# Graph network kernel, second aggregation pass: counts on four column groups, fourteen block buffers, two blocks kept in place

## The reference, cut to what matters

```python
def hyp_agg(x, src, dst, w, c, n_nodes):          # once in each of the two layers
    xt = logmap0(x, c)
    msg = xt[src] * w[:, None]
    agg = jax.ops.segment_sum(msg, dst, num_segments=n_nodes)
    return proj(expmap0(agg, c), c)
...
edge_features = jnp.concatenate([x[src], x[dst]], axis=-1)
h = jax.nn.relu(edge_features @ W1 + b1)
edge_out = h @ W2 + b2
agg = jax.ops.segment_sum(edge_out, dst, num_segments=n)
counts = jax.ops.segment_sum(jnp.ones_like(dst, dtype=edge_out.dtype), dst, num_segments=n)
return agg / jnp.clip(counts, 1.0)[:, None]
```

## Time and the profile before

| | |
|---|---|
| median of three runs | 1223.57 us (1220.88 to 1223.95) |
| the profiled execution | 1225.43 us |
| its span, first to last instruction | 1223.6 us |
| TensorE busy | 1063.2 us, 87% of the span |
| VectorE busy | 1001.1 us, 82% |
| ScalarE busy | 669.2 us, 55% |
| DMA traffic | 171.75 MB, 140 GB/s over the span |

### The profile page before, as it was taken

One profiled execution on the slowest core, in us unless ns is written; L12 is line 12 of the kernel. 1 busy time (PEld: TensorE's weight loads), 2 busy tenths in 40 slices (PEclk: granted clock), 3 DMA queues, 4 the chain that ended last, 5 costly groups with the idle time before them and its releaser, 6 DMA issues.

```text
span 1223.6 us, 53479 instructions
## 1 busy us (share of the span) xinstructions
PE 1063.2 (87%) x21956; PEld 984.6 (80%) x21956; DVE 1001.1 (82%) x1477; ACT 669.2 (55%) x1837; POOL 27.5 (2%) x28
## 2 busy tenths in 40 slices
PE   2079989898898988559999579999999999999997
PEld 2057877777777777358999559999999999999997
DVE  8789999999999997465554868888888888888884
ACT  5348888888888887300001475555555555555552
POOL 7000000000000000100000000000000000000000
PEclk9579999999999999769999679999999999999999
DMA  2003232222323223439991244444444445444440
GB/s 79 0 32 124 92 122 99 115 118 96 122 92 122 108 106 123 183 140 372 354 371 35 86 149 159 157 156 156 156 156 156 156 157 158 157 158 155 159 149 29
DMA packets 45160, 171.75 MB, mean 140 GB/s; under 512 B 19472, under 2 KB 19798, under 8 KB 45115
## 3 DMA queue, kind: packets, MB, share of 16 engines
q1 hardware_dynamic: 45115, 171.12, 39.2%
HBM read 122.95 MB, written 48.14 MB: 140 GB/s over the span
## 4 chain that ended last, share of the span: by engine, by line
PE 53%; DVE 32%; issue 8%; DVEq 4%; ACT 3%; DMA 0%; POOL 0%; POOLq 0%; ACTq 0%
PE PS L1475 17%; PE PS L1477 11%; DVE arena L985 8%; PE PS L1495 7%; PE PS L1354 7%; DVE arena L962 5%; PE PS L1490 5%; DVE arena L970 4%; DVE arena L948 3%; PE PS L1382 3%; DVE arena L957 2%; DVEq L344 2%; PE PS L1430 1%; DVE Cw L777 1%; DVE rows L777 1%
## 5 line engine op out<-in xcount | busy, mean ns | idle before, releaser
L1475 PE MATMUL PS<-arena 125*128 125x128 bf16 x3600 | 344.9, 219 | 6.3 <-ACT RT L714 6.2
L1475 PEld LDWEIGHTS PS<-arena 125*128 125x128 bf16 x3600 | 250.6, 97 | 11.2 <-issue 7.3
L1354 PE MATMUL PS<-arena,A 125*64 125x72 f32 x4800 | 178.1, 229 | 69.1 <-DVE aggTw L996 40.2
L1354 PEld LDWEIGHTS PS<-arena,A 125*64 125x64 f32 x4800 | 164.4, 138 | 78.7 <-DVE A L866 27.0
L609 ACT ACTIVATE arena<-arena 128x72 bf16<-128x72 bf16 x864 | 216.9, 343 | 2.1 <-DVE arena L970 2.1
L728 ACT ACTIVATE arena<-PS 128x512 bf16<-128x512 f32 (+2 forms) x336 | 172.2, 543 | 82.6 <-PE PS L1477 82.5
L721 ACT ACTIVATE arena<-arena 128x512 bf16<-128x512 f32 x144 | 90.9, 631 | 153.8 <-DVE arena L1198 153.7
L1477 PE MATMUL PS<-arena 108*128 108x128 bf16 x1200 | 167.6, 221 | 0.0
L1477 PE MATMUL PS<-arena,HTw 108*128 108x128 bf16 x1200 | 165.8, 219 | 0.0
L1339 PE MATMUL PS<-arena 128*128 128x72 bf16 x3600 | 126.9, 199 | 0.0
L1339 PEld LDWEIGHTS PS<-arena 128*128 128x128 bf16 x3600 | 120.8, 101 | 4.9
(11 more groups left out here) (188 smaller groups left out, 1458.3 us busy)
## 6 DMA issues: line engine op xcount, KB each, us to landing
adjacency<-arena SPq DMA_DIRECT2D x48, 900.0 KB, 3.6
arena<-adjacency SPq DMA_DIRECT2D x48, 900.0 KB, 4.8
Bw<-slot_rows SPq DMA_DIRECT2D x48, 800.0 KB, 4.1
Cw<-slot_rows SPq DMA_DIRECT2D x48, 700.0 KB, 4.4
arena<-q_table SPq DMA_DIRECT2D x144, 18.0 KB
q_table<-arena SPq DMA_DIRECT2D x6, 336.0 KB
slot_rows<-slot_row SPq DMA_DIRECT2D x49, 13.0 KB
x_sb<-in_x SPq DMA_DIRECT2D x1, 700.0 KB
```

The source lines that it names most:

```text
L1354: last = mm(sums[half, :], A[:, b, :], adjacency[0:PN, b, :], start=(b < 2), stop=(b >= NB - 2))
L1475: mm(ps, OTs[k][:, b, :], P3[:, b, part, :], start=(part == 0), stop=False)
```

## The change

The counts of tile t go to partitions 32 (t mod 4) to 32 (t mod 4) + 31, with 32 columns of ones as the stationary operand, so that four partial counts stand on four quarters of the partitions. `degree` is then all of `RT`, and the product at the end (line 1437) adds the four with the vector `first_of` (ones on partitions 0, 32, 64 and 96), in two halves of the nodes. The counts have two PSUM buffers, and wait for the additions of the group two before. VectorE makes the one-hots of group g + 1 in step g. `OC` and `offb` move from the arena into `Cw`. The arena gives 14 block buffers in place of six. SyncE issues the loads of groups 0 to 5 and then 38 to 45 without waiting, and then those of 6 to 37 through six buffers. Groups 46 and 47 are read from `AB[0]` and `AB[1]`, and not loaded. The order is 6 groups written out, a loop of five iterations over six groups, and 12 groups written out.

```diff
+EARLY = 8
+LOOPED = NG - EARLY - 2
...
-        degree = RT[0:1, :]
+        degree = RT[:, :]
...
+        starts = list(range(0, kept - NB * W + 1, NB * W)) + list(range(at[0], ARENA - NB * W + 1, NB * W))
...
-        cnt_ps = bank(3)[0:1, 0:W]
+        cnt_ps = [bank(2 + k)[:, 0:W] for k in range(2)]
...
-            whole = (NG - SECOND) // SECOND - 1
-            first = NG - whole * SECOND
-            for g in range(first):
+            for g in range(SECOND):
+                body(g, g, 0, g % 2)
+            rounds = LOOPED // SECOND
+            with eng.Fori(1, rounds) as j:
+                for r in range(SECOND):
+                    body(SECOND * j + r, r, j, r % 2)
+            for g in range(rounds * SECOND, LOOPED):
                 body(g, g % SECOND, g // SECOND, g % 2)
-            with eng.Fori(0, whole) as j:
-                for i in range(SECOND):
-                    g = first + i
-                    body(SECOND * j + g, g % SECOND, j + g // SECOND, g % 2)
+            for g in range(LOOPED, NG - 2):
+                body(g, SECOND + g - LOOPED, 0, g % 2)
+            for g in range(NG - 2, NG):
+                body(g, None, 0, g % 2)
...
+            def load_second():
+                for g in range(SECOND):
+                    load_blocks(g, g)
+                for g in range(LOOPED, NG - 2):
+                    load_blocks(g, SECOND + g - LOOPED)
+                rounds = LOOPED // SECOND
+                with sp.Fori(1, rounds) as j:
+                    for r in range(SECOND):
+                        sp.wait_ge(applied2, nth(SECOND * (j - 1) + r))
+                        load_blocks(SECOND * j + r, r)
+                for g in range(rounds * SECOND, LOOPED):
+                    sp.wait_ge(applied2, nth(g - SECOND))
+                    load_blocks(g, g % SECOND)
...
+            ve.tensor_reduce(first_of[:, :], ident[:, 0:128:32], X, ALU.add)
...
-                def body(g, _, n, k):
-                    ve.wait_ge(cone_set, nth(g - 2))
+                def count_onehots(g, k):
+                    ve.wait_ge(counted, nth(g - 2))
                     nc.vector.tensor_copy(offb[k], offT[:, bass.ds(g * GT, GT)].unsqueeze(2)
...
                     ve.wait_ge(cdloc_set, nth(g))
-                    ve.wait_ge(counted, nth(g - 2))
...
+                def body(g, at_k, n, k):
+                    if not is_last(g):
+                        count_onehots(g + 1, 1 - k)
                     base = window(ve, g)
...
-                    nc.vector.tensor_tensor(win, win, cnt_ps, ALU.add).then_inc(added2, 1)
+                    nc.vector.tensor_tensor(win, win, cnt_ps[k], ALU.add).then_inc(added2, 1)
...
-                apply(applied2, agg2_ps[k], ABS[blocks_at])
+                apply(applied2, agg2_ps[k], AB[k] if at_k is None else ABS[at_k])
                 pe.wait_ge(cone_set, nth(g))
-                pe.wait_ge(added2, 2 * g + PRIMED)
+                if from_third(g):
+                    pe.wait_ge(added2, 2 * g - 2 + PRIMED)
                 for t in range(GT):
-                    last = mm(cnt_ps, onesb[:, 0:1], OC[k][:, t, :], start=(t == 0), stop=(t == GT - 1))
+                    quarter = slice(32 * (t % 4), 32 * (t % 4) + 32)
+                    last = mm(cnt_ps[k][quarter, :], onesb[:, 0:32], OC[k][:, t, :], start=(t < 4), stop=(t >= GT - 4))
...
-                last = mm(PS[0:PN, 3584 + b:3585 + b], degree[:, 0:N].rearrange("f (p b) -> f b p", b=NB)[:, b, :],
-                          ones[0:1, 0:1], start=True, stop=True)
+                for ps in node_halves:
+                    last = mm(PS[ps, 3584 + b:3585 + b], degree[:, 0:N].rearrange("f (p b) -> f b p", b=NB)[:, b, ps],
+                              first_of[:, :], start=True, stop=True)
```

More of the change, by code:

```diff
@@ L121, in gnn_kernel @@
         y2s = sb("y2s", [128, 2])
+        first_of = sb("first_of", [128, 1])
         oki = sb("oki", [1, 2], i32)
@@ L150, in gnn_kernel @@
         AB = [carve(NB * W).rearrange("p (b w) -> p b w", w=W) for _ in range(2)]
[L152 to L155, removed]
+        kept = at[0] - 2 * NB * W
+        starts = list(range(0, kept - NB * W + 1, NB * W)) + list(range(at[0], ARENA - NB * W + 1, NB * W))
+        assert len(starts) >= SECOND + EARLY
+        ABS = [arena[:, i:i + NB * W].rearrange("p (b w) -> p b w", w=W) for i in starts[0:SECOND + EARLY]]
+        OC = [Cw[:, i * GT * HW:(i + 1) * GT * HW].bitcast(bf16).rearrange("p (t w) -> p t w", w=W) for i in range(2)]
+        offb = [Cw[:, 2 * GT * HW + i * GT:2 * GT * HW + (i + 1) * GT].bitcast(bf16).rearrange("p (t d) -> p t d", d=2)
+                for i in range(2)]
         fieldT = carve(TILES * FIELDS, bf16).rearrange("p (t f d) -> p t f d", f=FIELDS, d=2)
@@ L272, in gnn_kernel @@
         a_stored = sem("a_stored")
-        a_in = [sem(f"a_in{k}") for k in range(SECOND)]
+        a_in = [sem(f"a_in{k}") for k in range(SECOND + EARLY)]
         applied2, added2, counted, cdloc_set, cone_set = (counts(n) for n in (
@@ L387, in store_rows, with load_blocks @@
                     .then_inc(row_stored, 16)
-            def load_blocks(g, k, n, c):
-                if not (isinstance(g, int) and g < SECOND):
-                    sp.wait_ge(applied2, nth(g - SECOND))
+            def load_blocks(g, k):
                 sp.dma_start(ABS[k].rearrange("p b w -> p (b w)"),
                              a_d[bass.ds(g, 1), :, :].rearrange("g p w -> (g p) w")).then_inc(a_in[k], 16)
+            def load_second():
[11 more added lines that the diff above has]
+                    load_blocks(g, g % SECOND)
             def any_indices(i):
@@ L416, in _ @@
                     with sp.If(fast == 1):
-                        second_groups(sp, load_blocks)
+                        load_second()
             def load_sources(g):
@@ L1058, in body @@
                     win = degree[:, bass.ds(base, W)]
-                    nc.vector.tensor_tensor(win, win, cnt_ps, ALU.add).then_inc(added2, 1)
+                    nc.vector.tensor_tensor(win, win, cnt_ps[k], ALU.add).then_inc(added2, 1)
+                count_onehots(0, 0)
                 second_groups(ve, body)
@@ L1105, in any_order @@
                         if i < 2:
-                            win = degree[:, bass.ds(v * W, W)]
+                            win = degree[0:1, bass.ds(v * W, W)]
                             nc.vector.tensor_tensor(win, win, any_ps[F:F + 1, :], ALU.add)
@@ L1372, in first_body, with second_body @@
                 blocks(g, k)
-            def second_body(g, blocks_at, n, k):
-                pe.wait_ge(a_in[blocks_at], 16 * (n + 1))
-                if not (isinstance(g, int) and g < 2):
+            def second_body(g, at_k, n, k):
+                if at_k is not None:
+                    pe.wait_ge(a_in[at_k], 16 * (n + 1))
+                if from_third(g):
                     pe.wait_ge(added2, 2 * g - 3 + PRIMED)
-                apply(applied2, agg2_ps[k], ABS[blocks_at])
+                apply(applied2, agg2_ps[k], AB[k] if at_k is None else ABS[at_k])
                 pe.wait_ge(cone_set, nth(g))
-                pe.wait_ge(added2, 2 * g + PRIMED)
+                if from_third(g):
+                    pe.wait_ge(added2, 2 * g - 2 + PRIMED)
                 for t in range(GT):
-                    last = mm(cnt_ps, onesb[:, 0:1], OC[k][:, t, :], start=(t == 0), stop=(t == GT - 1))
+                    quarter = slice(32 * (t % 4), 32 * (t % 4) + 32)
+                    last = mm(cnt_ps[k][quarter, :], onesb[:, 0:32], OC[k][:, t, :], start=(t < 4), stop=(t >= GT - 4))
                 last.then_inc(counted, 1)
```

## The result

The changed kernel takes 1207.47 us (median of six runs, 1204.48 to 1211.02), the kernel before 1223.76 us in the same runs. The ratio is 0.9866, 95% interval 0.9851 to 0.9880: 16.3 us faster, or 1.3%. Forecast were 1204.5 us, 18.9 us faster.

The account below looks back on a forecast made before the run. TensorE's own row of matmuls was taken to bound the stretch. The terms 19.0 + 1.0 - 0.5 - 0.5 - 0.1 gave 18.9 us gained, from 1223.6 to about 1204.5 us, range 1201 to 1216.

Parts of the forecast that it names:

- What bounds the stretch: From the end of `linear` to the transposes, 533.39 to 656.5 us: TensorE's own matmuls set the pace, 2.453 us a group.
- Counts on four column groups: The 17 counts of each group: four quarters stream at once, 0.395 us gained a group, 19.0 us over 48; chance 0.70.
- the floor near 31 ns: Rival on the counts: a floor per matmul of 31.2 ns leaves 2.6 us gain there, 1220.6 us in all; chance 0.16.
- the Trainium skill's 25 ns: Counts: starts never closer than about 25 ns would give 7.4 us in place of 19.0, kernel 1215.8 us.
- One-hots a group ahead: VectorE's one-hots at the loop's five later returns: 0.2 us each no longer lost, 1.0 us gained.
- More code written out: 24 bodies in place of 18: stalls at the loop's first iteration stay at 1.9 us, leaving the loop costs 0.5.
- Loads: Block loads of the stretch: the ring keeps up with 3.4 us to spare through early loads; 0.5 us lost to delays.
- Small parts: Clearing `RT`, transposed counts and `first_of`: nothing gained from the faster transposed counts, 0.1 us lost at the reduction to `first_of`.

Follow-up runs that it names:

- x6_one_quarter: Changed kernel with all 17 counts on the first quarter, still 32 columns of ones, so everything but the column groups; one run of 1222.79 us.
- x3_counts_first: Changed kernel with each group's counts ahead of its product (group 0 excepted) and VectorE adding counts first; 1206.74 us, ratio 0.9862.
- x8_onehots_in_step: Changed kernel with the one-hots of a group made in its own step again, as before; 1208.46 us, ratio 0.9864.
- x5_counts_alone: Kernel before with only the four column groups added, keeping one PSUM buffer of counts and all loads and loops; 1215.13 us, ratio 0.9919.
- x1_no_ring: Changed kernel without the loads of groups 6 to 37, which reuse what the six buffers held (sums left wrong); one run of 1204.29 us.
- x10_six_looped: Changed kernel with six buffers and all 48 blocks loaded, the loop running to the end with no code behind it; 1210.43 us, ratio 0.9889.
- x7_six_buffers: Changed kernel without early and kept blocks: six buffers, all 48 blocks loaded, same order of bodies; 1215.8 us, ratio 0.9943.
- x12_halves_warm: Changed kernel with only group 0 ahead of the loop, counts before products, small warming matmuls, and two halves for four quarters; 1201.87 us, ratio 0.9816.
- x2_loop_early: Changed kernel with only group 0 written out ahead of the loop, and six iterations over groups 1 to 36; 1203.64 us, ratio 0.9842.

## Why the prediction was right, point by point

- **What bounds the stretch** was read rightly: TensorE's own row of matmuls. The column groups make 0.39 of the 0.42 us by which its pace changed, and without them the change is worth nothing that can be told from chance (x6_one_quarter).
- **Counts on four column groups**: forecast 0.415 less 0.02 us a group, 19.0 us; measured 2.453 less 2.035, 0.418 x 48 = 20.1 us. The starts are 8.7 ns apart on average. So neither the floor near 31 ns nor the Trainium skill's 25 ns ("TensorE: Matmul & The Clock Gate", section "Wait — 56ns, not 53.3ns?") holds for matmuls on different column groups; within one quarter x6_one_quarter has 33 ns, with 32 columns of weights as with one before. That this is the 72 columns' own stream is likely and not shown.
- **One-hots a group ahead**, +1.0 us: wrong in sign. VectorE's late one-hots at the five returns (0.2 us each) did go. In their place TensorE's own return shows, 0.34 to 0.36 us at each of the four that are left, because 0.14 us of counts no longer cover it: the returns cost 1.4 us where they had cost 1.0, so 0.4 us are lost in place of 1.0 won. x6_one_quarter has the slow counts and the one-hots ahead, and its returns cost nothing: the term was right for the old counts and failed with the new. x3_counts_first removes the loss, and x8_onehots_in_step shows that the step ahead gives nothing with fast counts.
- **More code written out**: the mis-sized term. I kept the stalls at the loop at 1.9 us and gave 0.5 for its exit. The exit cost 0.1, and the first block read from `AB` another 0.1. From group 5 to the end of the first iteration 6.3 us were lost, 1.6 of them at the lower clock behind the longest stop: 4.4 us more than before. My argument, that twelve bodies ran without a stall, held for the old pace. x5_counts_alone has those twelve bodies at the new pace, and stops among them. x1_no_ring shows that the loads are needed for it: without them 0.8 us are lost in place of the 6.3.
- **Loads**: the ring kept up, and no product waited for a block; the 0.5 us set aside weren't used. But what I named as the use of the early and kept blocks was not it: six buffers keep up too (x10_six_looped). They are worth 8 to 9 us in this order of bodies (x7_six_buffers, 1215.8 to 1207.5, ratios 0.9943 and 0.9866), as it seems because they leave the DMA engines free while twelve new bodies are fetched. That they helped at the exit was luck: the prediction had no such use for them.
- **Small parts**: the transposed counts take 6.23 us, forecast 6.3, and TensorE then waits 19.70 us for VectorE in place of 13.90, so nothing was gained, as said. `linear` ends 42.0 us after the first load was issued in both, so eight more loads beside it cost nothing.

```profile
648.18 6.23 PE L1469 MATMUL PS<-first_of,RT 128*61 128x1 f32 x99
674.10 4.93 PE L1315 MATMUL PS<-ident,A 125*64 125x125 f32 x25 [19.70 <-DVEq L1189]
```

The sum by these terms: 20.1 - 0.4 for returns (1.4 now, 1.0 before) - 4.4 - 0.2 - 0.1 at the start = 15.0 us, against 14.9 between the stretches. The forecast had put its 18.9 us there. So the mechanism that carries the gain was read rightly, and two smaller terms, returns and stalls, were wrong by 1.4 and 4.4 us, against 1.1 us more from the column groups. The whole came nearer, 16.3 of 18.9 us, because some 1.8 us of difference lie outside the stretch in the profiled pair, which no term had and no run explains.

That instructions come late is inferred: the trace shows stops without a wait, in code that runs for the first time, only while loads run. Their transfers are seen (queue q8), but not which one a stop waited for. The stops stand at the same rows in several kernels (group 7 behind row 42 or 43, group 11 behind row 24 to 27), which fits instructions that arrive in blocks and fits no wait for data.

## What to carry to other kernels

Small matmuls with few output rows gained here from column groups by the number of groups, but count the changes between products with different groups: using the same groups as the neighbours shortened the group by 0.09 us here against using more, though no median shows it (x12_halves_warm). When a stage gets faster, look at what its length had covered: the loop's return, the transfers of its own instructions, the clock. Code that runs for the first time beside saturated loads cost 6.3 us in the changed kernel and about 12 in x5_counts_alone; a loop over it (x10_six_looped), less of it ahead of the loop's return (x2_loop_early), or loads moved away from it (the changed kernel against x7_six_buffers) won a part of such losses back.

## What the runs showed of the hardware

- Matmuls on four different 32-column groups started 8.7 ns apart on average, against 33 ns on one.
- Between matmuls on 64-column and on 32-column groups lay about 0.28 us for the two changes of a group, usual distances of starts included; with equal groups product and counts interleaved, and a group was 0.09 us shorter though its counts took 0.2 us more.
- TensorE stopped for 0.3 to 2.8 us at a time inside code that it ran for the first time while the DMA engines were at 0.9 to 1.0, for 0.17 us without that traffic (x1_no_ring, share 0.02), and not at all in later iterations of the same loop, at a share of 1.0.
- After a stop of 2.36 us the granted clock fell to 0.50, its lower level (1.2 GHz), and a product took 3.38 us in place of 1.84. The same happened behind stops of 1.93 to 2.81 us in seven other kernels here, and not behind those of 2.36, 2.40 and 2.46 us in x7_six_buffers and of 2.33 us in x3_counts_first (granted clock 1.00).
- A return of the loop cost TensorE 0.34 us behind 17 counts that start within 0.14 us, and nothing behind a product (1.6 us) or behind 17 counts that start within 0.53 us (x6_one_quarter).
